# Normalising the rows of attention on ScalarE, with a scale and a bias per row, instead of on VectorE

## The chip, the cores and the metric

One core of one Trainium2 chip runs the whole program. Its engines are PE (TensorE, matrix products), DVE (VectorE), ACT (ScalarE), POOL (GpSimd) and SP (SyncE, which here only issues transfers). Each works through its own list of instructions in order, and they meet at semaphores. The metric is the device time of one execution in microseconds (us).

## The reference, cut to what matters

Three residual blocks act on x of 16 sequences of 256 tokens with 128 features, in fp32: half a mixture-of-experts feed-forward, one attention-like block, and half a feed-forward again. Each reads a layer-normalised x. The change touches the layer norm ahead of the middle block:

```
def _layernorm(x, axis=-1, eps=1e-05):
    m = jnp.mean(x, axis=axis, keepdims=True)
    v = jnp.var(x, axis=axis, keepdims=True)
    return (x - m) / jnp.sqrt(v + eps)
...
x = x + 0.5 * _L0_ffn_ref(_layernorm(x, axis=-1), ...)
x = x + _L0_attn_ref(_layernorm(x, axis=-1), ...)     # the layer norm in question
x = x + 0.5 * _L0_ffn_ref(_layernorm(x, axis=-1), ...)
```

The middle block multiplies its normalised input (scaled again by its root mean square) with the weights for q, k and v, normalises q and k, sums exp(k) and exp(k)*v along the sequence, divides the sums, multiplies by sigmoid(q), and passes the result through a gated product and an output projection. It adds its own input, the normalised rows, so those are used twice: by the product for q, k, v, and by a residual addition.

## The kernel before, in words

A token sits on one of 128 partitions. A tile is 128 tokens by 128 features, and x stays in SBUF in X as 32 tiles. The attention part works on 16 batches, one sequence of two tiles each (TB = 2). It lies between the two feed-forward parts: the first ends with results that come back from DRAM and are added to X by POOL; the second starts when the last batch has been added to X (at_added).

The attention is a software pipeline written out per engine. A table for each engine (POOL_STAGES, DVE_STAGES, ACT_STAGES, PE_STAGES, lines 69 to 75) lists its stages in the order in which a step issues them, each with a lag. In step k, a stage of lag d works on batch k - d. The function pipelined (line 123) writes this out step by step. No planner decides anything: the order in the lists is the order of the engines, and a stage that waits holds up all that stands behind it.

The way of one batch: at_statistics and at_aggregate (DVE) take mean and variance of each row; at_rsqrt (POOL, line 664) raises the variance to the power -0.5 into at_rstd; at_normalise (DVE, line 1060) makes xn in two instructions, one for each tile: subtract the mean, multiply by at_rstd. transpose_xn (PE, 1539) and copy_anT (ACT, 1254) turn it; qkv (PE, 1547) makes q, k, v in PSUM; squares (ACT, 1263) sums their squares; qkv_rsqrt (POOL, 699) makes the factors at_fac; weights (ACT, 1273 and 1276) takes exponential and tanh with them; weigh_v (DVE, 1068) multiplies by v; cumulate (PE, 1557 to 1559) makes the running sums; denominator (ACT, 1286), then invert (DVE, 1076), scale_q (1080) and attend (1088) divide them; transpose_y, copy_yT and swiglu make the gated product; tanh_g (ACT, 1297), gate_g and gate_u (DVE, 1094 and 1101) gate it; project (PE, 1589) and add_attention (DVE, 1108) add it to X. residual (POOL, 687) adds xn to X. add_routed (POOL, 592 and 594) adds the results of the feed-forward before.

The order of one step on DVE is: at_normalise(k-4), at_aggregate(k-3), gate_g(k-8), at_statistics(k-2), gate_u(k-8), invert(k-6), scale_q(k-6), weigh_v(k-5), attend(k-6), add_attention(k-9). On ACT it is: tanh_g(k-8), denominator(k-6), copy_yT(k-7), copy_anT(k-4), weights(k-5), squares(k-4). On PE: cumulate(k-6), transpose_y(k-7), project(k-9), transpose_xn(k-4), qkv(k-4), swiglu(k-7). Steps 16 to 19 and some later ones begin on DVE with statistics and normalisation for the second feed-forward (LN_STEPS, ln_ahead), four tiles a chunk. xn, at_rstd and at_mv have two buffers.

Of the kernel before, what the change touches and what calls it, by code (L numbers as in the profile page):

```python
# [13 lines left out]
P = 128  # L14
# [11 lines left out]
TB = SEQ // P  # L26
# [40 lines left out]


POOL_STAGES = [("qkv_rsqrt", 5), ("residual", 5), ("at_rsqrt", 3), ("mean_square", 4), ("add_routed", 1)]
DVE_STAGES = [("at_normalise", 4), ("at_aggregate", 3), ("gate_g", 8), ("at_statistics", 2), ("gate_u", 8),  # L70
              ("invert", 6), ("scale_q", 6), ("weigh_v", 5), ("attend", 6), ("add_attention", 9)]
ACT_STAGES = [("tanh_g", 8), ("denominator", 6), ("copy_yT", 7), ("copy_anT", 4),
              ("weights", 5), ("squares", 4)]
PE_STAGES = [("cumulate", 6), ("transpose_y", 7), ("project", 9), ("transpose_xn", 4), ("qkv", 4),
             ("swiglu", 7)]
# [3 lines left out]
for c in range(CHUNKS - 1):  # L79
    added = CH // TB * (c + 1) + dict(DVE_STAGES)["add_attention"]  # L80
    LN_STEPS.setdefault(max(BATCHES + max(c - 1, 0), added), []).append(c)
# [14 lines left out]
ALU = mybir.AluOpType  # L96
ACT = mybir.ActivationFunctionType
# [25 lines left out]
def pipelined(eng, stages, count, unroll, guard=2, at=None, straight=False):  # L123

    deepest = max(d for _, d in stages)
    head = count if straight else -(-(deepest + guard) // unroll) * unroll

    def static(k):  # L130
        if at and k in at:
            at[k]()
        for stage, d in stages:
            i = k - d
            if 0 <= i < count:
                stage(Step.of(i, unroll))

    for k in range(min(head, count)):
        static(k)
    if count > head:  # L140
        with eng.Fori(0, (count - head) // unroll) as r:
            for u in range(unroll):
                for stage, d in stages:
                    k = head + u - d
                    stage(Step(r + k // unroll, k % unroll, unroll, k))
    for k in range(count, count + deepest):
        static(k)
# [15 lines left out]
def macaron(nc, x, w_qkvT, w_swigluT, w_outT, gateT, w1_e, w3_e, w2_e, w1_s, w3_s, w2_s, out):  # L163
    ctx = ExitStack()
    with ctx:
        def sb(name, shape, dt=fp32):
            return ctx.enter_context(nc.sbuf_tensor(name, shape, dt))
# [4 lines left out]
        def sem(name):  # L172
            return ctx.enter_context(nc.semaphore(name))
# [18 lines left out]
        X = sb("X", [P, TILES, D])  # L192
# [59 lines left out]
        at_mv = sb("at_mv", [P, 2, TB, 2])  # L252
        at_var = sb("at_var", [P, 2, 2, TB])
        at_rstd = sb("at_rstd", [P, 2, TB])
        at_sq = sb("at_sq", [P, 2, TB])
        at_eps = sb("at_eps", [P, 2, 2, TB])
        at_ms = sb("at_ms", [P, 2, 3, TB])
        at_fac = sb("at_fac", [P, 2, 3, TB])
# [68 lines left out]
        xn = memory["xn"]  # L327
# [95 lines left out]
        sq_link = sem("sq_link")  # L423
        rms_terms = sem("rms_terms")
        at_scaled = sem("at_scaled")
        xn_ready = sem("xn_ready")
        xres_done = sem("xres_done")
        anT_psum = sem("anT_psum")
# [288 lines left out]
        def _(dve):  # L717
# [34 lines left out]
            for l in range(2):  # L752
# [296 lines left out]
                    dve.tensor_scalar(at_var[:, s.u, 0, :], at_mv[:, s.u, :, 1], LN_EPS, None, ALU.add)\  # L1049
                       .then_inc(at_stat, 1)  # L1050

                def at_normalise(s):

                    dve.wait_ge(at_scaled, s.i + 1)
                    if s.past(2):
                        dve.wait_ge(anT_psum, s.i - 1)
                        dve.wait_ge(xres_done, s.i - 1)
                    for t in range(TB):
                        xt = X[:, bass.ds(s.i * TB + t, 1), :].rearrange("p a d -> p (a d)")
                        i = dve.tensor_scalar(xn[:, s.u, t, :], xt, at_mv[:, s.u, t, 0:1],  # L1060
                                              at_rstd[:, s.u, t:t + 1], ALU.subtract, ALU.mult)
                    i.then_inc(xn_ready, 1)

                def weigh_v(s):

# [38 lines left out]
                def add_attention(s):  # L1104
# [4 lines left out]
                       .then_inc(at_added, 1)  # L1109

                stages = {"weigh_v": weigh_v, "gate_u": gate_u, "add_attention": add_attention,
                          "at_normalise": at_normalise, "at_statistics": at_statistics, "attend": attend,
                          "at_aggregate": at_aggregate, "invert": invert, "scale_q": scale_q, "gate_g": gate_g}

                def ln_ahead(chunks):
                    def run():
                        for c in chunks:
                            stats(1, Step.of(c, 2))
                            if c > 0:
                                normalise(1, Step.of(c - 1, 2))  # L1120
                    return run

                pipelined(dve, [(stages[n], d) for n, d in DVE_STAGES], BATCHES, 2, straight=True,
                          at={k: ln_ahead(chunks) for k, chunks in LN_STEPS.items()})
# [3 lines left out]
        def _(act):  # L1128
            act.wait_ge(consts, CONSTS)
            for l in range(2):  # L1130
# [116 lines left out]
                if l == 1:  # L1247
                    continue

                def copy_anT(s):  # L1250
                    act.wait_ge(anT_psum, s.i + 1)
                    if s.past(2):
                        act.wait_ge(qkv_psum, s.i - 1)
                    act.activation(anT[:, s.u % 2, :], psT[:, 0:TB * P], ACT.Copy).then_inc(anT_done, 1)
# [40 lines left out]
                def tanh_g(s):  # L1295
                    act.wait_ge(uv_psum, s.i + 1)
                    act.activation(tg[:, s.u % 2, :], psU[:, 1, 256:512], ACT.Tanh, scale=0.5).then_inc(tg_done, 1)

                stages = {"copy_yT": copy_yT, "tanh_g": tanh_g, "weights": weights, "copy_anT": copy_anT,
                          "squares": squares, "denominator": denominator}  # L1300
                def copy_turned(c):

# [10 lines left out]
                def ahead(k):  # L1313
                    def run():
                        for c in TURNED_STEP.get(k - 1, ()):
                            copy_turned(c)
                        for c in SCORED_STEP.get(k - 1, ()):
                            copy_scores(c)
                    return run

                act_end = BATCHES + max(d for _, d in ACT_STAGES)
                pipelined(act, [(stages[n], d) for n, d in ACT_STAGES], BATCHES, 4, straight=True,
                          at={k: ahead(k) for k in range(act_end)})
# [340 lines left out]
```

## Time and profile before

| | |
|---|---|
| runs, median (lowest to highest) | 748.2 us (746.82 to 748.32) |
| profiled execution: its own time, its span | 750.38 us, 748.7 us |
| mean granted TensorE clock | 0.963 |
| busy share of the span: PE, DVE, ACT, POOL | 89%, 62%, 55%, 59% |

```profile
## 2 busy tenths in 40 slices
PE   3878929999999999966887777999999999999996
DVE  6678884555444555447999885975455545454435
ACT  2658504666666666326664526663666666666520
POOL 5600396677777777459997515006577777777530
PEclk9989959999999999989999997999999999999998
```

A slice is a fortieth of the span, some 18.7 us; a digit is the busy share in tenths (9 is 90% or more), and in the last line the clock that TensorE was granted, in tenths of full speed. The attention takes the slices in the middle in which PE falls to 6 to 8 and DVE rises to 9. Outside the attention the feed-forward parts run, with PE at 9 nearly throughout.

In the rows further on, "L1060" is line 1060 of the kernel before, out<-in names the tiles written and read, and xN counts instructions.

### The profile page before, as it was taken

What the parts mean: (1) busy time and instruction counts of PE and PEld (TensorE: products, weight loads), DVE (VectorE), ACT (ScalarE), POOL (GpSimd) and SP (SyncE); (2) the same over time, 40 slices, a digit from 0 to 9 for tenths busy, and PEclk for the clock granted to TensorE, in tenths of its full rate; (3) what the DMA queues carried; (4) which work ended last, traced back from release to release, by engine and by line L of the source; (5) the groups of instructions that cost most, each with busy time, mean ns of one, the idle gap of its engine ahead of it and who ended that gap; (6) DMA issues with size and microseconds to landing.
All of it is one profiled execution on the core that took longest, in us unless ns stands there. A gap on an engine that the chain in (4) does not pass through costs nothing.

```text
span 748.7 us, 14295 instructions
## 1 busy us (share of the span) xinstructions
PE 664.1 (89%) x4860; PEld 604.9 (81%) x4860; DVE 463.5 (62%) x1169; ACT 411.0 (55%) x861; POOL 445.3 (59%) x519
## 2 busy tenths in 40 slices
PE   3878929999999999966887777999999999999996
PEld 3667829999999999944664565788999999999973
DVE  6678884555444555447999885975455545454435
ACT  2658504666666666326664526663666666666520
POOL 5600396677777777459997515006577777777530
PEclk9989959999999999989999997999999999999998
DMA  9551001112222132031100000602121221112146
GB/s 299 217 88 27 2 15 44 43 50 55 53 53 54 51 55 54 30 123 42 42 30 1 0 1 1 116 2 44 36 55 55 51 54 51 54 53 52 39 130 228
DMA packets 35686, 45.91 MB, mean 61 GB/s; under 512 B 6433, under 2 KB 27937, under 8 KB 35233
## 3 DMA queue, kind: packets, MB, share of 16 engines
q1 hardware_dynamic: 25632, 24.39, 11.5%
q0 software_dynamic: 9984, 20.63, 11.3%
q8 instruction: 40, 0.66, 0.4%
q14 instruction: 30, 0.24, 0.1%
HBM read 28.41 MB, written 16.58 MB: 60 GB/s over the span
## 4 chain that ended last, share of the span: by engine, by line
PE 66%; DVE 20%; ACT 3%; issue 3%; POOL 3%; DMA 2%; SPq 1%; POOLq 0%; DVEq 0%; ACTq 0%
PE psY L1487 18%; PE psU L1336 6%; PE psU L1335 6%; PE psU L1334 6%; PE psG L1334 6%; PE psG L1336 6%; PE psG L1335 6%; PE psH L1405 5%; DVE rec L1076 3%; PE psT L1433 2%; DVE XN L747 2%; DVE hs L757 2%; DVE ln_stats L734 1%; DVE xn L1060 1%; POOL results L650 1%
## 5 line engine op out<-in xcount | busy, mean ns | idle before, releaser
L1155 ACT ACTIVATE silu<-psG 128x512 f32<-128x512 f32 x220 | 131.1, 596 | 168.3 <-PE psG L1336 147.9
L635 POOL DMA_INDIRECT rows<-tokens,source x156 | 150.3, 964 | 104.4 <-issue 45.3
L954 DVE TENSOR_TENSOR hT<-silu,psU 128x512 f32<-128x512 f32 x156 | 107.4, 688 | 157.9 <-PE psU L1336 151.5
L650 POOL DMA_INDIRECT results<-yout,target x156 | 153.4, 983 | 64.0 <-issue 45.7
L1487 PE MATMUL psY<-W,hT 128*128 x1232 | 162.3, 275 | 1.8 <-DVE yout L980 1.8
L1487 PEld LDWEIGHTS psY<-W,hT 128*128 128x128 f32 x1232 | 150.4, 191 | 2.1 <-DVE hT L954 2.1
L1229 ACT ACTIVATE w_high<-W13H 128x1024 fp32r x78 | 82.7, 1060 | 55.5 <-PE psU L1336 55.4
L1334 PE MATMUL psG<-xTH,w_high 128*128 128x256 f32 x312 | 100.0, 321 | 0.0
L1336 PE MATMUL psG<-xTH,w_low 128*128 128x256 f32 x312 | 88.0, 282 | 0.0
L1336 PE MATMUL psU<-xTH,w_low 128*128 128x256 f32 x312 | 88.0, 282 | 0.0
L1335 PE MATMUL psU<-xTL,w_high 128*128 128x256 f32 x312 | 87.7, 281 | 0.0
L1335 PE MATMUL psG<-xTL,w_high 128*128 128x256 f32 x312 | 87.4, 280 | 0.0
L1334 PE MATMUL psU<-xTH,w_high 128*128 128x256 f32 x312 | 86.9, 278 | 0.0
L1229 ACT ACTIVATE w_low<-W13L 128x1024 fp32r x78 | 81.8, 1048 | 0.0
L757 DVE TENSOR_TENSOR hs<-silu,psU 128x512 f32<-128x512 f32 x64 | 43.7, 685 | 45.9 <-PE psU L1336 38.0
L1405 PEld LDWEIGHTS psH<-W2S,hs 128*128 128x128 f32 x512 | 59.4, 192 | 4.1 <-DVE hs L757 2.6
L1405 PE MATMUL psH<-W2S,hs 128*128 128x128 f32 x512 | 60.0, 275 | 1.7 <-DVE hs L757 1.7
L1335 PEld LDWEIGHTS psG<-xTL,w_high 128*128 128x128 f32 x312 | 59.3, 190 | 0.0
L1334 PEld LDWEIGHTS psG<-xTH,w_high 128*128 128x128 f32 x312 | 59.2, 190 | 0.0
L1334 PEld LDWEIGHTS psU<-xTH,w_high 128*128 128x128 f32 x312 | 59.1, 190 | 0.0
L1336 PEld LDWEIGHTS psG<-xTH,w_low 128*128 128x128 f32 x312 | 58.8, 188 | 0.0
L1335 PEld LDWEIGHTS psU<-xTL,w_high 128*128 128x128 f32 x312 | 58.6, 188 | 0.0
(188 smaller groups left out, 1245.3 us busy)
## 6 DMA issues: line engine op xcount, KB each, us to landing
W<-w_e SPq DMA_DIRECT2D x3, 2048.0 KB, 13.8
tokens<-XN SPq DMA_DIRECT2D x16, 260.0 KB, 6.0
Y<-results SPq DMA_DIRECT2D x32, 128.0 KB, 2.2
YF<-results SPq DMA_DIRECT2D x16, 256.0 KB, 5.7
rows<-tokens,source POOLq DMA_INDIRECT x156
results<-yout,target POOLq DMA_INDIRECT x156, 2.3
X<-x SPq DMA_DIRECT2D x8, 256.0 KB, 5.5
out<-X SPq DMA_DIRECT2D x8, 256.0 KB, 2.8
```

What stands on the lines that cost most here:

```text
L635: pool.indirect_dma_start(rows[:, slot(l, g), t, :], None, tokens, bass.IndirectOffsetOnAxis(ap=source[:, tile:tile + 1], axis=0))\
L650: pool.indirect_dma_start(results, bass.IndirectOffsetOnAxis(ap=target[:, tile:tile + 1], axis=0), yout[:, g % 2, t, :], None).then_inc(y_ ...
L757: dve.tensor_tensor(hidden, silu[:, s.u % 2, :], psU[:, s.u % 2, :], ALU.mult).then_inc(h_done, 1)
L954: dve.tensor_tensor(hT[:, s.u // PT % 2, half, :].rearrange("p f c -> p (f c)"), silu[:, s.u % 2, :], psU[:, s.u % 2, :], ALU.mult).then_i ...
L1076: dve.reciprocal(rec[:, s.u, :, :], den[:, s.u, :, :]).then_inc(y_link, 1)
L1155: act.activation(silu[:, s.u % 2, :], psG[:, s.u % 2, :], ACT.Silu).then_inc(silu_done, 1)
L1229: act.activation(used[p % 2][:, :, :], kept[:, :, bass.ds(entries[p], F)], ACT.Copy)\
L1334: pe.matmul(out, a_high, b_high, start=True, stop=False)
L1335: pe.matmul(out, a_high, b_low, start=False, stop=False)
L1336: return pe.matmul(out, a_low, b_high, start=False, stop=True)
L1405: i = pe.matmul(psH[:, par, t * D:(t + 1) * D], hs[:, par, f, t * P:(t + 1) * P], W2S[:, f, :], start=(f == 0), stop=(f == FT - 1))
L1487: i = pe.matmul(into[:, t * D:(t + 1) * D], hT[:, s.u // PT % 2, f, s.u % PT * P:(s.u % PT + 1) * P], W2[:, bass.ds(at + f * D, D)], start ...
```

## The change

DVE's stage at_normalise becomes at_centre: one instruction a batch that writes at_shift = -mean * at_rstd for the batch's two tiles (128 partitions by 2 numbers). A new ACT stage at_normalise, first in ACT's list and of the same lag 4, writes xn = Identity(at_rstd * X + at_shift), one instruction for each tile, with scale and bias read per partition. Two waits (the buffer of xn has been transposed and added) go along to ACT; ACT waits for the new semaphore shift_made, and DVE's at_centre waits with xn_ready until the old at_shift has been read. Readers of xn (transpose_xn, residual) wait for the same semaphore xn_ready as before.

```diff
-DVE_STAGES = [("at_normalise", 4), ("at_aggregate", 3), ("gate_g", 8), ("at_statistics", 2), ("gate_u", 8),
+DVE_STAGES = [("at_centre", 4), ("at_aggregate", 3), ("gate_g", 8), ("at_statistics", 2), ("gate_u", 8),
               ("invert", 6), ("scale_q", 6), ("weigh_v", 5), ("attend", 6), ("add_attention", 9)]
-ACT_STAGES = [("tanh_g", 8), ("denominator", 6), ("copy_yT", 7), ("copy_anT", 4),
+ACT_STAGES = [("at_normalise", 4), ("tanh_g", 8), ("denominator", 6), ("copy_yT", 7), ("copy_anT", 4),
               ("weights", 5), ("squares", 4)]
...
-                def at_normalise(s):
+                def at_centre(s):
 
                     dve.wait_ge(at_scaled, s.i + 1)
                     if s.past(2):
-                        dve.wait_ge(anT_psum, s.i - 1)
-                        dve.wait_ge(xres_done, s.i - 1)
-                    for t in range(TB):
-                        xt = X[:, bass.ds(s.i * TB + t, 1), :].rearrange("p a d -> p (a d)")
-                        i = dve.tensor_scalar(xn[:, s.u, t, :], xt, at_mv[:, s.u, t, 0:1],
-                                              at_rstd[:, s.u, t:t + 1], ALU.subtract, ALU.mult)
-                    i.then_inc(xn_ready, 1)
+                        dve.wait_ge(xn_ready, s.i - 1)
+                    dve.scalar_tensor_tensor(at_shift[:, s.u, :], at_mv[:, s.u, :, 0], -1.0, at_rstd[:, s.u, :],
+                                             ALU.mult, ALU.mult).then_inc(shift_made, 1)
...
+                def at_normalise(s):
+
+                    act.wait_ge(shift_made, s.i + 1)
+                    if s.past(2):
+                        act.wait_ge(anT_psum, s.i - 1)
+                        act.wait_ge(xres_done, s.i - 1)
+                    u = s.u % 2
+                    for t in range(TB):
+                        i = act.activation(xn[:, u, t, :], X[:, s.i * TB + t, :], ACT.Identity,
+                                           scale=at_rstd[:, u, t:t + 1], bias=at_shift[:, u, t:t + 1])
+                    i.then_inc(xn_ready, 1)
```

## Rows read from the trace of the kernel before

**Rows 1.** Busy us (x instructions) by stretch: PE, PEld, DVE, ACT, POOL; clock, DMA.
```profile
358.90:391.50 32.60, 28.88 (x131) 20.70 (x130) 32.19 (x98) 20.88 (x96) 30.21 (x56) 1.00 0.12 38
```

**Rows 2.** Chain of waits (start us, us, what): DVE's reciprocal, one a step.
```profile
353.09 1.67 DVE rec L1076
358.95 1.67 DVE rec L1076
...
391.52 1.67 DVE rec L1076
```

**Rows 3.** The same chain, earlier: POOL's power instruction, one a step.
```profile
341.26 1.33 POOL at_fac L699
...
346.87 1.33 POOL at_fac L699
```

**Rows 4.** Timeline (start us, us, engine, line, operation): one step of DVE.
```profile
363.30 0.42 DVE L1094 SCALAR_TENSOR_TENSOR ag<-tg,psU 128x256 f32<-128x256 f32 x1
...
364.34 1.75 DVE L1076 RECIPROCAL rec<-den 128x256 f32<-128x256 f32 x1
...
366.99 0.41 DVE L1088 TENSOR_TENSOR ya<-ysc,psU 128x256 f32<-128x256 f32 x1
367.31 0.42 DVE L1108 SCALAR_TENSOR_TENSOR X<-psY,X 128x256 f32<-128x256 f32 x1
367.65 0.63 DVE L1060 TENSOR_SCALAR xn<-X,at_mv,at_rstd 128x128 f32<-128x128 f32 x2
...
368.62 0.41 DVE L1094 SCALAR_TENSOR_TENSOR ag<-tg,psU 128x256 f32<-128x256 f32 x1
```

**Rows 5.** Timeline of PE and ACT in the same step: cumulate, denominator, next cumulate, tanh_g.
```profile
362.06 0.67 PE L1557 MATMUL psU<-wkv,upto 128*128 128x256 f32 x2 [0.23 <-DVE ya L1088]
...
363.64 0.38 ACT L1286 ACTIVATE den<-psU 128x256 f32<-128x256 f32 x1 [1.21 <-PE psU L1559]
...
367.54 0.67 PE L1557 MATMUL psU<-wkv,upto 128*128 128x256 f32 x2
...
367.88 0.40 ACT L1297 ACTIVATE tg<-psU 128x256 f32<-128x256 f32 x1
```

**Rows 6.** Groups by line, 358.9 to 391.5 us: count, busy us, mean ns, idle before.
```profile
L1049 DVE TENSOR_SCALAR at_var<-at_mv 128x2 f32<-128x2 f32 x6 | 1.0, 160 | 0.0
...
L1263 ACT ACTIVATE sq<-psG 128x128 bf16<-128x128 f32 x12 | 3.2, 277 | 1.8 <-PE psG L1547 1.8
...
L1273 ACT ACTIVATE wkv<-psG,at_fac 128x128 f32<-128x128 f32 x6 | 1.9, 366 | 0.0
```

**Rows 7.** Timeline of ACT: the first exponentials and tanhs of the attention.
```profile
337.35 0.62 ACT L1273 ACTIVATE wkv<-psG,at_fac 128x128 f32<-128x128 f32 x2
337.86 0.62 ACT L1276 ACTIVATE tq<-psG,at_fac 128x128 f32<-128x128 f32 x2
```

**Rows 8.** Timeline: an ACT instruction that waited for DVE (second feed-forward).
```profile
474.01 0.48 DVE L875 TENSOR_TENSOR in_tile<-column,pos_part 128x312 bf16<-128x312 bf16 x1
...
474.52 0.56 ACT L1165 ACTIVATE pair<-in_tile,partition 128x312 bf16<-128x312 bf16 x1 [3.18 <-DVE in_tile L875]
```

**Rows 9.** Timeline of DVE: xn and gate_g in steps 16 and 19.
```profile
398.54 0.60 DVE L1060 TENSOR_SCALAR xn<-X,at_mv,at_rstd 128x128 f32<-128x128 f32 x2
...
399.48 0.42 DVE L1094 SCALAR_TENSOR_TENSOR ag<-tg,psU 128x256 f32<-128x256 f32 x1
...
421.52 0.60 DVE L1060 TENSOR_SCALAR xn<-X,at_mv,at_rstd 128x128 f32<-128x128 f32 x2
422.03 0.41 DVE L1094 SCALAR_TENSOR_TENSOR ag<-tg,psU 128x256 f32<-128x256 f32 x1
```

**Rows 10.** Timeline at the attention's start: first xn, its transposes, the table load.
```profile
328.69 1.55 DVE L1060 TENSOR_SCALAR xn<-X,at_mv,at_rstd 128x128 f32<-128x128 f32 x2 [0.41 <-POOL at_rstd L664]
...
330.39 0.66 PE L1539 MATMUL psT<-ident,xn 128*128 128x128 f32 x2 [4.84 <-DVE xn L1060]
...
335.92 1.28 ACT L1273 ACT_TABLE_LOAD   x1
```

More of the change, by code:

```diff
@@ L255, in macaron @@
         at_sq = sb("at_sq", [P, 2, TB])
+        at_shift = sb("at_shift", [P, 2, TB])
         at_eps = sb("at_eps", [P, 2, 2, TB])
@@ L425, in macaron @@
         at_scaled = sem("at_scaled")
+        shift_made = sem("shift_made")
         xn_ready = sem("xn_ready")
@@ L1111, in _ @@
                 stages = {"weigh_v": weigh_v, "gate_u": gate_u, "add_attention": add_attention,
-                          "at_normalise": at_normalise, "at_statistics": at_statistics, "attend": attend,
+                          "at_centre": at_centre, "at_statistics": at_statistics, "attend": attend,
                           "at_aggregate": at_aggregate, "invert": invert, "scale_q": scale_q, "gate_g": gate_g}
@@ L1297, in tanh_g @@
                     act.activation(tg[:, s.u % 2, :], psU[:, 1, 256:512], ACT.Tanh, scale=0.5).then_inc(tg_done, 1)
-                stages = {"copy_yT": copy_yT, "tanh_g": tanh_g, "weights": weights, "copy_anT": copy_anT,
+                stages = {"at_normalise": at_normalise, "copy_yT": copy_yT, "tanh_g": tanh_g, "weights": weights, "copy_anT": copy_anT,
                           "squares": squares, "denominator": denominator}
```

## The prediction

> **What bounds the kernel now.** The page's slices come first: PE is busy nearly everywhere but in the stretch from about 325 to 456 us, the attention, and the diff touches nothing outside it. What is gained or lost in it passes on whole, since the second feed-forward part starts from the last batch. Next, the busy time by stretch: from 358.9 to 391.5 us DVE works 32.19 of 32.60 us, POOL 30.21, PE 28.88 and ACT 20.88 [rows 1]. So DVE is full, POOL stands at 5.04 us a step (six steps), and ACT has time to spare. Then the chain of waits, where a step can be measured: the reciprocals that DVE runs once a step start 5.86 us apart at first (353.09 to 358.95) and then 5.43 apart (six steps to 391.52) [rows 2]. Before that the chain runs over POOL, whose power instruction comes every 5.61 us [rows 3]. From 391.5 on, the next layer's normalisation is put between the batches on DVE.
>
> Busy shares would say: take 0.6 us a step from the full engine, give it to the idle one, gain. The order of work says otherwise. The reader should see one DVE step in the timeline: gate_g at 363.30, add_attention at 367.31, the two instructions xn at 367.65, the next gate_g at 368.62 [rows 4]. gate_g reads what ACT's tanh wrote, and that tanh ran early: at 367.88, right behind the squares, while DVE was still busy with xn [rows 5]. That slack is what the change spends.
>
> **The change, part by part.** DVE loses two instructions a batch (xn, 0.60 us where undisturbed, [rows 9]) and gets one on 128x2. No row shows that form; the nearest is the 128x2 at_var instruction, 160 ns [rows 6]. I take 0.17; between 0.10 and 0.25 it moves the sum by at most 0.08 a step.
>
> ACT gets two ACTIVATEs of 128x128 a batch with scale and bias read per row. Squares of that size with no such operand take 277 ns, the exponential with one takes 366 [rows 6], so an operand costs 0.09 and I estimate 0.455 with two. A pair with one operand lets the next instruction start after 0.51 (337.35 to 337.86, [rows 7]); with a second operand on each I take 0.69 to the next start and 0.80 to the pair's end. The ends: 0.51, if the second operand costs nothing, and 1.00, if it costs double and the overlap goes. I take 0.69, as the measured operand is the nearest row.
>
> The Trainium skill ("ScalarE: Activation LUTs", What ACT_TABLE_LOAD costs) states 186 ns plus 0.833 ns an element plus 93 ns for each such operand, 93 ns of it overlapped. By this a pair would hold its successor for 0.77, and the sum below would be 0.9 us more; the exponential's 366 ns lies below the 386 that the rule gives for it, so the rows decide.
>
> The new wait is worth more than either. ACT's list now opens each step with at_normalise, which waits for DVE's at_centre, and tanh_g is queued behind it, with denominator, copy_yT, copy_anT, weights and squares behind that. DVE reaches at_centre only after add_attention of the step before, and soon after it needs tanh for gate_g. Counted from gate_g's start: 4.01 to add_attention and 0.34 more to where xn began [rows 4], 0.17 for at_centre, 0.03 from DVE to ACT (474.49 to 474.52, [rows 8]), 0.69 for the pair, 0.40 for tanh [rows 5], 0.03 back (taken the same): **5.67 us** a step, against 5.43. On DVE, the 0.97 between the old xn and gate_g held, behind xn, only some 0.4 of at_aggregate (0.94 in the steps that have it less 0.51 in the one that has not, [rows 9]), so about 0.6 becomes idle time; behind gate_g stand at_statistics, gate_u and the reciprocal, so all of it is late. In the undisturbed stretch that is 6 x 0.24 = +1.44 us. The 5.86 step just before held an xn pair slowed by POOL; it falls to 5.67, -0.19.
>
> A second loop lies close. From PE's first cumulate to ACT's tanh is 5.82 (362.06 to 367.88); with the pair, tanh and the hand-over it is 6.94; gate_g to the end of attend is 4.10 [rows 4], and cumulate follows 0.14 later [rows 5]. That is 11.18 for two steps, 5.59 each: below 5.67, so it adds nothing. The floor without either is cumulate to denominator (1.58, [rows 5]), its 0.38, a hand-over, 3.06 from the reciprocal to attend's end [rows 4], and 0.14: 5.19.
>
> In the four steps with normalisation ahead, the distance from xn's start to gate_g is 0.94 (398.54 to 399.48; three steps alike) and 0.51 in the last (421.52 to 422.03), which has no statistics left [rows 9]. After the change it is 0.17 + 0.03 + 0.69 + 0.40 + 0.03 = 1.32: +0.38 three times and +0.81 once, **+1.95**. The copies and the exponential behind xn move by the same 0.4 as gate_g and weigh_v do, so they meet as before.
>
> At the start the first xn pair took 1.55 us beside POOL's additions [rows 10]; at_centre and the ACT pair take 0.17 + 0.03 + 0.80 = 1.00, so the first batch is 0.55 sooner. In the next step, though, ACT normalises batch 1 only after the squares of batch 0, and copy_anT waits for that and for PE's two transposes (0.66, [rows 10]); behind them stand the table load (335.92, 1.28, [rows 10]) and the first exponential. That one comes 0.80 + 0.66 + 0.05 - 0.55, about 1.0, later in ACT's list, of which some 0.15 was waiting anyway: +0.8. POOL's 5.61 step was the limit here, and the 5.19 loop recovers 0.4 of it in each of one and a half steps before the first gate_g. I take **+0.2**. The ends are -2.2 (POOL stays the limit, keeps the 0.55, and falls to its 5.04 for three steps) and +0.8. POOL gets nothing new: residual reads xn a step later, and its buffers' waits are met by then.
>
> Sum: +0.2 - 0.19 + 1.44 + 1.95 = **+3.4 us**. Against the profiled execution (750.38 us, a span of 748.7) that is 753.8. That execution lies 2.2 above the median of the runs, 748.2, so the forecast for the median is **751.6**.
>
> **Rivals.** *The pair is cheap.* If the second operand hides and the pair holds tanh for only 0.51, a step is 5.49: +0.36, -0.37, 3 x 0.20 + 0.63 = +1.23, and the start at 0: +1.2, 749.4, inside what can be told from no change. For it: ACT's successive instructions overlap in the rows. Against: a single operand does show its 0.09.
>
> *The pair is dear.* With 1.00 for the pair a step is 5.98: +3.3, +0.12, 3 x 0.69 + 1.12 = +3.2, the start +0.5: +7.1, 755.3. No row shows two operands or this function, which speaks for it; two ACTIVATEs with one operand overlap, which speaks against.
>
> *Faster.* DVE's relief counts because tanh is not late. The place is gate_g: if tanh is there within the 0.6 us of at_centre and at_aggregate, the step falls to the 5.19 floor. That gives 6 x -0.24, -0.67 on the 5.86 step, 4 x -0.34 in the steps with normalisation and -0.55 at the start: -4.0, 744.2. It decides from where pair and tanh together take less than 0.4; tanh alone takes 0.40 [rows 5] and stands behind the pair, so it needs ACT to run them in another order than its list. POOL's freedom from xn is the one thing that speaks for part of it.
>
> *The table.* If the new function is not in the set loaded for exponential and tanh, each step has two loads more, 2 x 1.28 x 16 = 41 us: 789. Only one load stands in the attention now [rows 10]. The Trainium skill ("ScalarE: Activation LUTs", Table sets: the hidden batching unit) says that cheap functions, identity among them, are in every set; by that rule this rival is void, but no row of this trace shows the function.
>
> **How the numbers follow.** Forecast 0.55, with 750.0 to 753.5 as its own spread; cheap pair 0.24; dear pair 0.12; faster 0.07; table 0.02. About 0.2% (1.5 us) is what a measurement of this kernel can tell from no change. Slower: 0.55 + 0.12 + 0.02 = 0.69; same 0.24; faster 0.07. The range 747.8 to 755.0 takes in the cheap pair with a better start and most of the dear one.
>
> **What would show it.** Right: DVE idle before gate_g, released by ACT's tanh, some 0.6 us in each of about a dozen steps; reciprocals 5.6 to 5.75 apart; ACT's pair directly ahead of every tanh, waiting for at_shift; ACTIVATEs of 0.44 to 0.48. The first exponential later than 337.35 although the first transposes come sooner. Wrong: gate_g following at_aggregate without a gap, steps under 5.43, or table loads beside the new lines. A pair much shorter or longer than 0.69 would leave the mechanism and change the size.

## The result: 755.5 us, 1% slower, and twice the loss that was forecast

The changed kernel takes 755.51 us (median; 755.25 to 756.11) against 748.08: a ratio of 1.0098, 95% interval 1.0085 to 1.0111, or +7.4 us. The forecast was 751.6, in a range up to 755.0. The direction was right and the wait that was named is there; three sizes were wrong.

The profiled execution of the changed kernel (756.11 us) has the same busy shares as before to within a point. First the head and engine line of its page:

```profile
span 754.4 us, 14325 instructions
...
PE 666.9 (88%) x4860; PEld 604.6 (80%) x4860; DVE 458.4 (61%) x1153; ACT 423.9 (56%) x893; POOL 445.1 (59%) x519
```

DVE works 5.1 us less than before (463.5) and ACT 12.9 more (411.0 before), and the span is 5.7 longer. Busy time says nothing here; the timeline does. One steady step of the changed kernel (start us, us, engine, line, operation; in brackets the idle time before it and what ended it), which answers to [rows 4] and [rows 5]:

```profile
365.48 0.89 ACT L1256 ACTIVATE xn<-X,at_shift,at_rstd 128x128 f32<-128x128 f32 x2
...
366.25 0.39 ACT L1307 ACTIVATE tg<-psU 128x256 f32<-128x256 f32 x1
...
366.67 0.42 DVE L1092 SCALAR_TENSOR_TENSOR ag<-tg,psU 128x256 f32<-128x256 f32 x1 [0.91 <-ACT tg L1307]
...
369.33 0.73 POOL L594 TENSOR_TENSOR X<-X,Y 128x256 f32<-128x256 f32 x1
...
369.51 0.83 DVE L1078 SCALAR_TENSOR_TENSOR ysc<-tq,rec 128x256 f32<-128x256 f32 x1
...
371.45 0.15 DVE L1059 SCALAR_TENSOR_TENSOR at_shift<-at_mv,at_rstd 128x2 f32<-128x2 f32 x1
...
371.63 0.88 ACT L1256 ACTIVATE xn<-X,at_shift,at_rstd 128x128 f32<-128x128 f32 x2 [0.61 <-DVE at_shift L1059]
```

Two things are to be seen. DVE stood idle 0.91 us before gate_g (366.67), for tanh_g, which started when ACT's pair let it (365.48 to 366.25 is 0.77). And scale_q (ysc, 369.51), which reads two tiles in SBUF, began inside POOL's addition at 369.33 and took 0.83 us. The pair shown first waited for nothing: it began behind ACT's squares. The next one (371.63) waited 0.61 us for at_shift. The groups by line of the stretch from 358 to 400 us say how often (count, busy us, mean ns, idle before and its releaser), first of the kernel before, then after the change:

```profile
L1080 DVE SCALAR_TENSOR_TENSOR ysc<-tq,rec 128x256 f32<-128x256 f32 x7 | 3.0, 429 | 0.2
L1094 DVE SCALAR_TENSOR_TENSOR ag<-tg,psU 128x256 f32<-128x256 f32 x8 | 3.3, 413 | 0.0
```

```profile
L1256 ACT ACTIVATE xn<-X,at_shift,at_rstd 128x128 f32<-128x128 f32 x14 | 6.2, 488 | 2.0 <-DVE at_shift L1059 1.8
...
L1078 DVE SCALAR_TENSOR_TENSOR ysc<-tq,rec 128x256 f32<-128x256 f32 x8 | 5.1, 644 | 0.3
L1092 DVE SCALAR_TENSOR_TENSOR ag<-tg,psU 128x256 f32<-128x256 f32 x7 | 2.9, 421 | 5.6 <-ACT tg L1307 5.6
```

gate_g waits 0.8 us a step (5.6 us in seven), where before it waited for nothing, and scale_q's mean rose from 429 ns to 644. The start of the attention, in the same timeline view, answers to [rows 7] and [rows 10]:

```profile
325.31 0.73 POOL L594 TENSOR_TENSOR X<-X,Y 128x256 f32<-128x256 f32 x1 [3.96 <-DMA Y<-results]
...
329.25 0.70 DVE L1059 SCALAR_TENSOR_TENSOR at_shift<-at_mv,at_rstd 128x2 f32<-128x2 f32 x1 [0.40 <-POOL at_rstd L666]
...
329.98 0.88 ACT L1256 ACTIVATE xn<-X,at_shift,at_rstd 128x128 f32<-128x128 f32 x2 [8.55 <-DVE at_shift L1059]
...
336.11 0.89 ACT L1256 ACTIVATE xn<-X,at_shift,at_rstd 128x128 f32<-128x128 f32 x2
...
337.05 0.44 PE L1549 MATMUL psT<-ident,xn 128*128 128x128 f32 x2 [1.99 <-ACT xn L1256]
...
337.93 1.28 ACT L1283 ACT_TABLE_LOAD   x1
...
339.23 0.63 ACT L1283 ACTIVATE wkv<-psG,at_fac 128x128 f32<-128x128 f32 x2
...
341.07 1.22 PE L1567 MATMUL psU<-wkv,upto 128*128 128x256 f32 x2 [1.02 <-DVE wkv L1066]
...
344.04 0.38 ACT L1296 ACTIVATE den<-psU 128x256 f32<-128x256 f32 x1 [1.60 <-PE psU L1569]
...
344.45 1.75 DVE L1074 RECIPROCAL rec<-den 128x256 f32<-128x256 f32 x1 [2.12 <-ACT den L1296]
```

The pair of batch 1 (336.11) stands behind the squares of batch 0; PE is idle 1.99 us for it, then copy_anT, the table load and the first exponential follow. From cumulate to denominator it is 2.97 us. The next two fences show the same part of the kernel before (timeline) and the granted clock of both (busy us by engine, then the clock before the last two numbers):

```profile
324.75 0.72 POOL L592 TENSOR_TENSOR X<-X,Y 128x256 f32<-128x256 f32 x1 [3.97 <-DMA Y<-results]
...
339.18 0.70 PE L1557 MATMUL psU<-wkv,upto 128*128 128x256 f32 x2 [1.67 <-DVE wkv L1068]
...
340.78 0.38 ACT L1286 ACTIVATE den<-psU 128x256 f32<-128x256 f32 x1 [1.27 <-PE psU L1559]
...
341.46 1.74 DVE L1076 RECIPROCAL rec<-den 128x256 f32<-128x256 f32 x1
```

Before:

```profile
340.00:348.00 8.00, 4.68 (x20) 2.82 (x18) 6.30 (x18) 3.83 (x17) 7.53 (x13) 1.00 0.13 40
```

After:

```profile
340.00:348.00 8.00, 5.36 (x14) 3.25 (x13) 5.41 (x17) 5.22 (x27) 6.31 (x12) 0.64 0.12 37
```

There the same span from cumulate to denominator was 1.60 us, at the full clock (1.00, the 2.4 GHz level); after the change it was 2.97, at 0.64 on average (0.50, the 1.2 GHz level, from 340 to 344 us).

The loss by stretch, from the starts of DVE's reciprocals (one a step; the first is counted from POOL's first addition, in both kernels):

| us | before | after | difference | forecast |
|---|---|---|---|---|
| POOL's first addition to first reciprocal | 16.71 | 19.14 | +2.43 | +0.2 (*) |
| next three steps | 17.41 | 17.42 | +0.01 | -0.19 |
| six steady steps, each | 5.43 | 5.94 | 6 x 0.51 = +3.06 | +1.44 |
| four steps with normalisation ahead | 31.38 | 33.94 | +2.56 | +1.95 |

(*) The forecast's +0.2 is +0.8 at the first exponential less 0.6 that was to be recovered in the steps behind it.

The differences add up to 8.06; to the last add_attention the attention is 8.13 us longer (119.86 to 127.99 from POOL's first addition). The two profiled spans differ by only 5.7, since in the profiled execution of before what follows the attention took 3.0 us longer than after the change; PE was granted 0.61 there from 448 to 452 us. The runs' medians differ by 7.4.

### The profile page after: what moved, and what is told of

Its sections match the earlier page's. It is cut to its first block, busy times and chain, and to the rows that moved or that the text cites. A ratio compares the mean times of both kernels' runs of the same rounds, so it can differ in the third digit from the quotient of the medians.

```text
span 754.4 us, 14325 instructions
## 1 busy us (share of the span) xinstructions
PE 666.9 (88%) x4860; PEld 604.6 (80%) x4860; DVE 458.4 (61%) x1153; ACT 423.9 (56%) x893; POOL 445.1 (59%) x519
## 4 chain that ended last, share of the span: by engine, by line
PE 68%; DVE 18%; ACT 6%; issue 5%; DMA 2%; SPq 1%; POOL 1%; POOLq 0%; DVEq 0%; ACTq 0%
PE psY L1497 18%; PE psG L1344 6%; PE psU L1344 6%; PE psG L1345 6%; PE psG L1346 6%; PE psU L1345 6%; PE psU L1346 6%; PE psH L1415 5%; DVE rec L1074 3%; PE psT L1443 2%; DVE XN L749 2%; DVE hs L759 2%; DVE ln_stats L736 1%; ACT xn L1256 1%; ACT pair L1166 1%
## 5 line engine op out<-in xcount | busy, mean ns | idle before, releaser
L1346 PEld LDWEIGHTS psU<-xTH,w_low 128*128 128x128 f32 x312 | 58.9, 189 | 0.0
```

The source lines that it names most:

```text
L1346: return pe.matmul(out, a_low, b_high, start=False, stop=True)
```

## The experiments

All kernels start from the changed one but the fifth, and are compared with the kernel before on the same chip. The columns are those of the table above.

| kernel | to first reciprocal | steady step | four steps | ratio (95% interval) |
|---|---|---|---|---|
| before | 16.71 | 5.43 | 31.38 | 1 |
| the change | 19.14 | 5.94 | 33.94 | 1.0098 (1.0085 to 1.0111) |
| 1 tanh first | 18.88 | 5.39 | 30.43 | 1.0014 (1.0003 to 1.0024) |
| 2 at_centre early | 18.86 | 5.85 | 29.95 | 1.0041 (1.0026 to 1.0055) |
| 3 start on DVE | 16.95 | 5.83 | 33.92 | 1.0074 (1.0049 to 1.0099) |
| 4 scale_q from PSUM | 19.13 | 5.74 | 33.52 | 1.0090 (1.0072 to 1.0108) |
| 5 twin on ACT | 18.44 | 5.86 | 31.49 | 1.0052 (1.0036 to 1.0069) |
| 6 = 1 and 3 | 16.56 | 5.37 | 30.43 | 0.9982 (0.9973 to 0.9991) |
| 7 = 1, 2 and 3 | 16.72 | 5.39 | 29.67 | 0.9967 (0.9955 to 0.9978) |
| 8 batch 1 on DVE | 16.94 | 5.83 | 33.92 | 1.0067 (1.0054 to 1.0080) |

**1. tanh_g ahead of at_normalise.**

```diff
-ACT_STAGES = [("at_normalise", 4), ("tanh_g", 8), ("denominator", 6), ("copy_yT", 7), ("copy_anT", 4),
+ACT_STAGES = [("tanh_g", 8), ("at_normalise", 4), ("denominator", 6), ("copy_yT", 7), ("copy_anT", 4),
```

> The changed kernel with one edit: in ACT's list tanh_g stands ahead of at_normalise. Theory Q (queue: most of the loss in the steady steps is tanh_g waiting behind at_normalise, which waits for at_centre): gate_g follows at_aggregate without a gap, the reciprocals come 5.3 to 5.5 us apart instead of 5.94, and the four steps with normalisation ahead become shorter than in the kernel before, about 0.4 us each; the start still costs its 2.4. Sum about 748 + 2.4 - 0.5 - 1.7 = 748.3. Rival W (ACT's longer work, not its order): the step stays above 5.7 and the time above 752. Rival P (POOL's additions meeting scale_q): the reciprocals come about 5.6 apart, scale_q still near 640 ns, 750 to 752.

Two names swapped give back 6.3 of the 7.4 us. The step falls to 5.39, the four steps are 0.95 us shorter than before the change, the start keeps most of its loss. So the place of the pair ahead of tanh_g is the cause of most of the steady loss, as theory Q says, but the four steps gave 0.95 in all and not the 0.4 each that it expected. scale_q's mean fell to 432 ns in the same run, so the swap takes away both terms of the steady loss; experiment 4 parts them. The chain of waits (start us, us, what) then shows the next limit, one round of which is:

```profile
366.72 1.56 PE psG L1557 x4
368.28 0.86 PE psU L1590 x4
369.14 0.43 PE psU L1567 x2
...
371.23 0.42 PE psT L1549 x2
...
371.68 0.39 ACT anT L1264
...
372.12 1.56 PE psH L1557 x4
```

That is PE's own list of a step: qkv, swiglu, cumulate, the transposes, the projection, ACT's copy, and qkv again 5.40 us later. The kernel before, at 5.43, stood right above it.

**2. at_centre earlier on DVE.**

```diff
-DVE_STAGES = [("at_centre", 4), ("at_aggregate", 3), ("gate_g", 8), ("at_statistics", 2), ("gate_u", 8),
-              ("invert", 6), ("scale_q", 6), ("weigh_v", 5), ("attend", 6), ("add_attention", 9)]
+DVE_STAGES = [("at_aggregate", 3), ("gate_g", 8), ("at_statistics", 2), ("gate_u", 8),
+              ("invert", 6), ("at_centre", 3), ("scale_q", 6), ("weigh_v", 5), ("attend", 6), ("add_attention", 9)]
```

> The changed kernel with at_centre moved on DVE from the head of a step to behind the reciprocal of the step before (lag 3), so that at_shift is ready when ACT's squares end. Theory Q says the wait for at_centre is half of it: in the steps with normalisation ahead the ACT pair and tanh run while DVE normalises, and all of their +2.6 us and about 1.5 more come back; in the steady steps the loop over PE, squares, pair and tanh (5.6 to 5.65) takes over, about -0.3 a step. Sum 755.5 - 4.1 - 1.8 = about 749.6. Rival W: the pair's time on ACT alone is the cost, nothing changes in the steady steps, and the time stays above 753.

The four steps did as said (-4.0 us). The steady steps hardly did, 5.6 and 6.1 by turns, and the time is 751.3 us, not 749.6. scale_q met POOL's additions and took 0.82 to 0.86 us in seven of eight steps (group by line, 358 to 400 us):

```profile
L1078 DVE SCALAR_TENSOR_TENSOR ysc<-tq,rec 128x256 f32<-128x256 f32 x8 | 6.2, 780 | 0.1
```

**3 and 8. The start.** The third experiment leaves the first two batches to DVE:

```diff
+ON_DVE = 2
...
+                    if s.i < ON_DVE:
+                        for t in range(TB):
+                            i = dve.tensor_scalar(xn[:, s.u, t, :], X[:, s.i * TB + t, :], at_mv[:, s.u, t, 0:1],
+                                                  at_rstd[:, s.u, t:t + 1], ALU.subtract, ALU.mult)
+                        i.then_inc(xn_ready, 1)
+                        return
...
+                    if s.i < ON_DVE:
+                        return
+                    act.wait_ge(shift_made, s.i + 1 - ON_DVE)
```

> The changed kernel, with the first two batches normalised on DVE as in the kernel before and the other 14 on ACT. Theory S (the start lost 2.4 us because at_normalise of batch 1 stands behind the squares of batch 0, ahead of copy_anT, the table load and the first exponential, and PE's clock then falls): the first reciprocal comes 16.7 us after POOL's first addition, as before, not 19.1, PE's first cumulate is at full clock, and the time is 755.5 - 2.4 = 753.1. Rival: the steps after it are limited by something else and the gain is used up before the steady steps, 755.

The eighth leaves it batch 1 alone (s.i == 1, with a wait for batch 0's xn):

> The changed kernel with batch 1 alone normalised on DVE (batch 0 on ACT). Theory S says that batch 1 alone costs the start, since only it stands behind the squares of batch 0: the first reciprocal comes 16.9 us after POOL's first addition, within 0.3 of the third experiment, and the whole time is the same, about 754. Rival (the first batch's own way over ACT costs as much): about 18 us.

Timeline of the eighth:

```profile
323.95 0.73 POOL L595 TENSOR_TENSOR X<-X,Y 128x256 f32<-128x256 f32 x1 [3.95 <-DMA Y<-results]
...
340.89 1.75 DVE L1082 RECIPROCAL rec<-den 128x256 f32<-128x256 f32 x1 [0.24 <-ACT den L1306]
```

16.94 and 16.95 us: the whole loss of the start, but for 0.2 us, is removed by taking batch 1 from behind the squares of batch 0. The clock fell in these kernels too, only earlier, so that PE's first cumulate was not at full clock as the third experiment had expected (busy us by engine, then the clock, third experiment):

```profile
332.00:340.00 8.00, 6.61 (x15) 3.47 (x14) 1.85 (x10) 5.75 (x24) 5.64 (x11) 0.55 0.11 33
340.00:348.00 8.00, 5.07 (x21) 3.00 (x20) 7.28 (x16) 5.73 (x23) 7.61 (x14) 1.00 0.22 66
```

From 332 to 340 us 0.55 was granted here (0.81 before, 0.71 after the change). It lay on qkv of batch 1, which took 2.93 us instead of 1.56 before, and the cumulate to the denominator took 2.08 (third) and 2.03 (eighth), between 1.60 and 2.97. So 16.95 us is reached with the low clock on other work, and the start's two terms, the order and the clock, are removed together, not apart. Experiments 6 and 7 reach 16.56 and 16.72.

In time the third gained 1.3 us (754.23, single runs 751.1 to 756.3) and the eighth 2.1 (753.39, 752.9 to 753.4). The third's interval overlaps with the change's, the eighth's (up to 1.0080) lies below it (from 1.0085): a gain is shown in the whole time, but that it is the 2.2 us is shown at the first reciprocal only. In both profiles the step behind the four with normalisation took 7.44 us, at PE's lower level, where the changed kernel's took 5.74. So 1.7 us of the gain was lost again there.

**4. scale_q without a second operand in SBUF.**

```diff
-                    dve.scalar_tensor_tensor(ysc[:, s.u, :, :], tq[:, s.u, :, :], 1.0, rec[:, s.u, :, :],
+                    sums = psU[:, 0, :].rearrange("p (t a d) -> p t a d", t=TB, a=2)
+                    dve.scalar_tensor_tensor(ysc[:, s.u, :, :], sums[:, :, 0, :], 1.0, rec[:, s.u, :, :],
                                              ALU.add, ALU.mult).then_inc(y_link, 1)
```

> The changed kernel; scale_q reads the sums in PSUM in place of tanh(q) in SBUF, of the same size (the sigmoid of q is left out, other data stand for it). Theory P (POOL's additions hold up an instruction of DVE that reads two SBUF operands: scale_q rose from 429 to 644 ns): scale_q falls to about 430 in every step, the steady step from 5.94 to about 5.75, and the time by 1.3 to 2.0 us to 753.5 to 754.2. Rival: scale_q is late only where gate_g would wait anyway, and the time stays within 0.5 us of 755.5.

Group by line, 358 to 400 us:

```profile
L1079 DVE SCALAR_TENSOR_TENSOR ysc<-psU,rec 128x256 f32<-128x256 f32 x7 | 3.0, 424 | 0.2
```

scale_q is held up in none of these steps, and the last five steady steps are 5.71 or 5.72 each. The whole time, 755.75, did not follow: the step behind the four took 7.43 us at PE's lower clock here too, and single runs spread from 753.3 to 758.0. So the share of the steady step is shown, its worth in the whole time is not.

**5. ACT's work without the wait.** The kernel before, with a twin of the pair on ACT:

```diff
+                def twin(s):
+                    for t in range(TB):
+                        act.activation(scratch[:, t, :], ident[:, :], ACT.Identity,
+                                       scale=partition[:, 0:1], bias=minus_half[:, t:t + 1])
...
-ACT_STAGES = [("tanh_g", 8), ("denominator", 6), ("copy_yT", 7), ("copy_anT", 4),
+ACT_STAGES = [("twin", 4), ("tanh_g", 8), ("denominator", 6), ("copy_yT", 7), ("copy_anT", 4),
```

> The kernel before, DVE untouched, with two ACTIVATEs of the same form (scale and bias per row, 128x128, written to a tile that nobody reads) at the head of each of ACT's steps, waiting for nothing. They take ACT the same 0.79 us ahead of tanh_g that the change takes, but without the wait for at_centre. Theory Q (the wait matters, and the work itself only through the loop over PE, squares, pair, tanh and gate_g): the steady step is (5.82 + 0.79 + 0.40 + 0.03 + 4.10 + 0.14) / 2 = 5.64 instead of 5.43, the steps with normalisation ahead stay as before (31.4 us for four) because ACT has slack there, and the start loses about 0.5, since nothing is transposed late: +1.2 + 0 + 0.5, ratio about 1.002. Rival W (ACT's work as such): the steps with normalisation lose 2.6 too, and the ratio comes near 1.009.

Right in the four steps (31.49: no loss without the wait). In the steady steps it is 5.86, not 5.64, and the ratio is 1.0052, not 1.002. The timeline shows the loop that was expected, gate_g waiting for a tanh behind the twin, and on top of it the same delay of scale_q:

```profile
376.06 0.89 ACT L1303 ACTIVATE scratch<-ident,minus_half,partition 128x128 f32<-128x128 f32 x2
376.83 0.39 ACT L1299 ACTIVATE tg<-psU 128x256 f32<-128x256 f32 x1
377.25 0.42 DVE L1096 SCALAR_TENSOR_TENSOR ag<-tg,psU 128x256 f32<-128x256 f32 x1 [0.47 <-ACT tg L1299]
...
379.93 0.72 POOL L594 TENSOR_TENSOR X<-X,Y 128x256 f32<-128x256 f32 x1
380.08 0.84 DVE L1082 SCALAR_TENSOR_TENSOR ysc<-tq,rec 128x256 f32<-128x256 f32 x1
```

DVE still makes xn here, so what moves POOL's additions into scale_q is not the freed DVE. The start lost 1.7 us, more than the 0.5 expected. The first exponential came only 0.62 later than before (13.22 us from POOL's first addition, 12.60 before), but PE's first cumulate ran at the lower clock here as well, and from it to the denominator are the same 2.97 us:

```profile
340.20 1.22 PE L1564 MATMUL psU<-wkv,upto 128*128 128x256 f32 x2 [1.54 <-DVE wkv L1070]
...
343.17 0.38 ACT L1288 ACTIVATE den<-psU 128x256 f32<-128x256 f32 x1 [1.87 <-PE psU L1566]
```

So the two halves of theory Q come apart. In the four steps the loss comes with the wait for at_centre. In the steady steps it comes mainly with the place on ACT ahead of tanh_g: 0.79 us there cost a step 0.43 even without the wait (scale_q's delay included), and experiment 2, which takes the wait away, gave back only 0.09, though scale_q took 0.14 more there.

**6 and 7. What the experiments point to.** The sixth joins 1 and 3, the seventh adds 2.

> The changed kernel with tanh_g ahead of at_normalise on ACT and the first two batches normalised on DVE: the first and third experiments together. If the losses are separate they add up: the steady step 5.39 (there PE's own list is the limit), the four steps with normalisation 30.4 us, the start as in the kernel before: about 2.2 us under the first experiment, ratio to the kernel before 0.998. If the gain at the start is used up by PE's clock later, as it was in part in the third experiment, 1.000.

> As e6, with at_centre moved behind the reciprocal as well. The steady step cannot fall under PE's 5.38, so it stays at 5.39; the four steps with normalisation fall from 30.4 to about 29.9, as in the second experiment, because at_centre no longer stands behind the normalisation ahead: ratio about 0.997. Rival: in its new place at_centre and scale_q meet POOL's additions, the step is 5.5 or more, and nothing is gained over e6.

Both came out as expected: 746.86 us, and 745.43 against 748.16 of the kernel before (ratio 0.9967, 0.9955 to 0.9978), faster than the kernel before and the changed one. In the seventh the four steps took 29.67 us (reciprocals at 391.32 and 420.99).

## Why the prediction was wrong

**Right: the wait at gate_g.** DVE stands idle about 0.8 us a step for a tanh_g behind ACT's pair, and experiment 1 removes it by an order alone. Of the rivals, *The table* is out (one table load in the attention, as before). *The pair is dear* named 755.3 us, near the 755.5 measured, but by chance: the pair holds tanh_g for 0.79 us and not for 1.00. In the steps with normalisation ahead the account closes. From at_shift to gate_g the timeline of the last of them shows 1.37 us (1.32 forecast), waiting where the kernel before did not:

```profile
429.28 0.15 DVE L1059 SCALAR_TENSOR_TENSOR at_shift<-at_mv,at_rstd 128x2 f32<-128x2 f32 x1
...
430.65 0.42 DVE L1092 SCALAR_TENSOR_TENSOR ag<-tg,psU 128x256 f32<-128x256 f32 x1 [1.21 <-ACT tg L1307]
```

That is +0.43 three times and +0.86 once; the first two lost 0.2 each more through scale_q (0.63 and 0.59 us).

**Mis-sized a little: the pair.** "I take 0.69": it holds tanh_g for 0.77 to 0.79 (488 ns an instruction). The rule from the Trainium skill ("ScalarE: Activation LUTs", What ACT_TABLE_LOAD costs), which gave 0.77 and was set aside for the rows, agrees with the trace here: two operands were outside what the rows showed. With 0.79, the sum for a step is 4.01 + 0.34 + 0.15 + 0.03 + 0.79 + 0.37 + 0.03 = 5.72, and experiment 4 runs at 5.71 to 5.72. This term is 0.29 a step, not 0.24. Little of it is the wait for at_centre, which the prediction put first: without it the second loop of the prediction, over the squares, still gives 5.64 with 0.79 for the pair (the sum in the expectation of experiment 5).

**The step that failed first: "4.01 to add_attention" as a constant.** The sum carried DVE's chain over unchanged into a new rhythm. In the step shown above POOL's addition begins just ahead of scale_q (369.33 against 369.51); before the change it began just behind it (366.22 against 366.12). scale_q's mean is 425 to 432 ns in the kernels with steps of 5.43 and less (before, 1, 6, 7) and 542 to 780 in those with 5.83 and more (the change, 2, 3, 5, 8). That the longer step moves the additions is read from this order; no run sets it apart. What it costs is shown: 0.22 of the 0.51 a step, which experiment 4 takes away. The Trainium skill ("SBUF — State Buffer", SBUF: two separate sides) has the rule, that a DVE instruction with two SBUF inputs and a GpSimd instruction that reads SBUF lock each other out until the first is done. The trace agrees: 0.83 us beside an addition, 0.43 alone, and an addition that began together with scale_q (381.86) took 1.01 us instead of 0.73.

**The step that failed most: the start, "+0.2" for +2.43.** Its parts: the first batch was not 0.55 sooner, since at_shift itself took 0.70 us beside POOL's addition and xn was ready 5.55 us after POOL's first addition instead of 5.49. The first exponential came 1.32 later (13.92 against 12.60 from the same mark) instead of 0.8. Then the first cumulate fell into a stretch at the lower clock, to the denominator 2.97 against 1.60: +1.37, a term that the sum did not have; 0.26 of it all had been slack before the reciprocal. That PE's idle time ahead of it (1.99 us; 1.84 in experiment 5) brought the lower clock there is an order in time that holds in every kernel with the late first exponential: from 340 to 344 us the changed kernel and experiments 1, 2, 4 and 5 were granted 0.50, and the kernel before and 3, 6, 7 and 8 were granted 1.00. So the lower clock there goes with the late batch; no run separates the two, and what brings it stays open. And nothing was recovered: the next three steps took 17.42 us against 17.41.

**The floor of 5.19 holds only while the pipeline fills.** It stood behind that recovery and behind the rival *Faster*. The first step took 5.19 in experiments 3, 4 and 8; in the changed kernel it took 5.51, with scale_q at 0.74 us beside an addition. The second step, which has the first gate_g, took 6.07 to 6.09 in all four (5.94 before): there the chain runs over the squares, the pair and tanh_g. In the steady steps PE's list holds a step at 5.39, so a free DVE could win 0.04 at best; the 0.24 a step of *Faster* was never there. Experiments 1 and 7 win in the four steps with normalisation ahead, where DVE was busy 30.7 of 31.4 us before.

## What to carry to other kernels

A stage moved to an idle engine must be priced by what stands behind it in that engine's list: here swapping two names was worth 6.3 of 7.4 us. Look for the second-longest loop before counting the relief of the longest; it was 0.04 us away. And treat the first rounds of a pipeline apart, with their own order and PE clock.

## What was not expected of the hardware

An instruction of 128x2 elements on DVE took 0.70 us instead of 0.15 when it fell on a POOL addition, in the first step, and 0.46 to 0.65 us in the last three steady steps of experiment 1. PE's clock is below full for some 8 us in the start of every kernel here (before, 0.53 from 328 to 332 us and 0.61 to 336), and it was down once more where the batch came late: on the first cumulate in the changed kernel and in experiments 1, 2, 4 and 5 (1.22 us for its first two products, 0.70 before). In the changed kernel a first exponential 1.3 us late came out as a first reciprocal 2.4 us late. It also fell in the step after the four in experiments 3, 4 and 8 (7.4 us instead of 5.7). In the changed kernel it fell one batch earlier (0.57 from 424 to 428 us, qkv 2.89 us instead of 1.56), where the step took no longer for it (8.01; 8.00 in experiment 3). Why it falls there was not settled.
